# Groupnorm and attention on one core: scores of two rows in succession, and the order around them

## The reference

```python
x = x + attention(groupnorm(x))            # x: 16 images x 64 rows x 256 tokens x 128 channels, f32

groupnorm: mean and variance of each image over rows, tokens and the 4 channels of each of 32 groups
qkv   = einsum('bglc,dc->bgld', x, W_qkv) + b_qkv
score = softmax(einsum('bghlc,bghmc->bghlm', q, k) / sqrt(128))   # 2 heads of 64 channels, 256 x 256 each
out   = einsum('bghlm,bghmc->bghlc', score, v)
```

## Time and profile before

| | us |
|---|---|
| median of 3 runs | 3863.12 (3862.29 to 3874.12) |
| the profiled execution | 3873.13 |
| its span, first to last instruction | 3871.2 |
| PE busy | 3781.4 (98%) |
| DVE busy | 3778.0 (98%) |
| ACT busy | 3037.4 (78%) |
| POOL busy | 1787.6 (46%) |

### The profile page before, as it was taken

How to read it: one execution, slowest core, us unless ns; L and a number is a source line. 1 busy time by engine, 2 the same in 40 slices (tenths; PEclk the granted TensorE clock), 3 DMA queues, 4 the chain that set the end, 5 groups by cost and what they waited for, 6 DMA issues and landing times.

```text
span 3871.2 us, 126226 instructions
## 1 busy us (share of the span) xinstructions
PE 3781.4 (98%) x44133; PEld 2995.0 (77%) x44133; DVE 3778.0 (98%) x6114; ACT 3037.4 (78%) x8193; POOL 1787.6 (46%) x2065
## 2 busy tenths in 40 slices
PE   4999999999999999999999999999999999999998
PEld 2777777777777777777777777777777777777777
DVE  5999999999999999999999999999999999999999
ACT  2777888778888878778787877887878877888886
POOL 1444444444444444444444444444444444444444
PEclk9999999999999999999999999999999999999999
DMA  7999999999999999999999999999999999999999
GB/s 196 219 212 213 216 214 214 215 215 215 215 214 217 219 212 215 214 214 214 212 213 214 213 217 213 213 218 215 215 216 216 217 213 213 214 196 181 180 181 176
DMA packets 2442225, 813.91 MB, mean 210 GB/s; under 512 B 2179072, under 2 KB 2441600, under 8 KB 2441600
## 3 DMA queue, kind: packets, MB, share of 16 engines
q1 hardware_dynamic: 2311040, 679.97, 98.5%
q10 hardware_dynamic: 130560, 125.86, 12.5%
HBM read 134.42 MB, written 134.22 MB: 69 GB/s over the span
## 4 chain that ended last, share of the span: by engine, by line
PE 93%; DVE 2%; DMA 2%; issue 2%; POOL 1%; ACT 1%; SPq 0%; ACTq 0%; POOLq 0%; DVEq 0%
PE s_pair L271 27%; PE qk_bank L249 27%; PE o_bank L287 19%; PE v_bank L259 11%; PE xt_bank L241 6%; PE v_bank L256 3%; DMA pt_hi<-p_hi 1%; DVE first_bn L439 1%; DVE p_lo L410 1%; POOL p_hi L573 0%; ACT prob L367 0%; DVE neg_max L402 0%; DMA image<-in_x_dram 0%; SPq L207 0%; DVE o_norm L429 0%
## 5 line engine op out<-in xcount | busy, mean ns | idle before, releaser
L573 POOL TENSOR_SCALAR p_hi<-prob 128x1024 f16<-128x1024 f32 x1024 | 1073.1, 1048 | 2075.1 <-ACT prob L367 1827.4
L367 ACT ACTIVATE prob<-s_pair,neg_max 128x256 f32<-128x256 f32 x4096 | 1612.7, 486 | 18.3 <-issue 9.4
L410 DVE SCALAR_TENSOR_TENSOR p_lo<-prob,p_hi 128x1024 f16<-128x1024 f32 x1024 | 1477.4, 1443 | 50.6 <-POOL p_hi L573 26.3
L347 ACT ACTIVATE qk<-qk_bank,b_in 128x256 f32<-128x256 f32 x2048 | 860.3, 471 | 744.0 <-PE qk_bank L249 744.0
L402 DVE TENSOR_REDUCE neg_max<-s_pair 128x4 f32<-128x1024 f32 x1024 | 1238.6, 1210 | 20.3 <-PE s_pair L271 19.4
L271 PE MATMUL s_pair<-qk 64*128 64x256 f32 x8192 | 1164.5, 403 | 1.4 <-ACT qk L347 1.4
L249 PE MATMUL qk_bank<-xc,w_norm 128*128 128x256 f32 x4096 | 1160.7, 406 | 0.0
L249 PEld LDWEIGHTS qk_bank<-xc,w_norm 128*128 128x128 f32 x4096 | 695.3, 189 | 393.4 <-issue 335.6
L287 PE MATMUL o_bank<-v_hi,pt_lo 128*128 128x65 f16 x8192 | 850.2, 193 | 37.7 <-issue 25.5
L271 PEld LDWEIGHTS s_pair<-qk 64*128 64x128 f32 x8192 | 706.4, 186 | 220.0 <-issue 171.4
L287 PE MATMUL o_bank<-v_lo,pt_hi 128*128 128x65 f16 x8192 | 851.6, 194 | 0.0
(11 more groups left out here) (71 smaller groups left out, 1640.6 us busy)
## 6 DMA issues: line engine op xcount, KB each, us to landing
out_dram<-y_ring SPq DMA_DIRECT2D x512, 256.0 KB, 3.7
image<-in_x_dram ACTq DMA_DIRECT2D x480, 256.0 KB, 3.6
pt_hi<-p_hi SPq DMA_TRANSPOSE x1024, 4.1
pt_lo<-p_lo SPq DMA_TRANSPOSE x1024, 3.7
image<-in_x_dram SPq DMA_DIRECT2D x4, 2048.0 KB, 16.3
w_in<-in_L_conv_W_qkv_dram SPq DMA_DIRECT2D x1, 192.0 KB, 2.4
b_in<-in_L_conv_b_qkv_dram SPq DMA_DIRECT2D x3, 0.5 KB, 2.1
```

The lines of the kernel that those rows point to most:

```text
L347: ins = act.activation(qk[:, v % 2, t, :], qk_bank[:, t * TOK:(t + 1) * TOK], ACT.Identity, bias=b_in[:, t:t + 1])
L367: ins = act.activation(prob[:, m, c:c + TOK], s_bank[m][h][:, a * TOK:(a + 1) * TOK], ACT.Exp, bias=neg_max[:, m, h, a:a + 1])
L410: dve.scalar_tensor_tensor(out=p_lo[:, v % 2, :], in0=prob[:, v % 2, :], scalar=P_SCALE, in1=p_hi[:, v % 2, :], op0=ALU.mult, op1=ALU.subt ...
L573: pool.tensor_scalar(p_hi[:, v % 2, :], prob[:, v % 2, :], P_SCALE, 1.0, ALU.mult, ALU.mult).then_inc(phi_done, 1)
```

## The change

The diff, whole:

```diff
@@ -34,7 +34,7 @@
-    X_AHEAD = 2
+    X_AHEAD = 3
@@ -188,7 +188,7 @@
-                order(run, next_image)
+                order(run, next_image, i % 2)
@@ -221,10 +221,10 @@   (SP)
-            def order(run, next_image):
-                run(-2, transpose_low)
-                run(-7, store)
-                run(-1, transpose_high)
+            def order(run, next_image, odd):
+                run(-1, transpose_low)
+                run(-6, store)
+                run(0, transpose_high)
@@ -319,13 +319,15 @@   (PE)
-            def order(run, next_image):
-                run(0, scores)
-                run(+1, project_qk)
+            def order(run, next_image, odd):
+                if not odd:
+                    run(0, scores)
+                    run(+1, scores)
+                run(+2, project_qk)
                 run(0, project_v)
                 next_image(0)
                 run(-3, values)
-                run(+3, x_transpose)
+                run(+4, x_transpose)
@@ -375,12 +377,15 @@   (ACT)
-            def order(run, next_image):
+            def order(run, next_image, odd):
                 next_image(0)
-                run(-1, exponent, 0)
-                run(-1, exponent, 1)
-                run(+2, x_copy)
-                run(+1, qk_copy)
+                if not odd:
+                    run(+3, x_copy)
+                run(0, exponent, 0)
+                run(0, exponent, 1)
+                if odd:
+                    run(+3, x_copy)
+                run(+2, qk_copy)
                 run(0, v_high)
@@ -548,15 +553,18 @@   (DVE)
-            def order(run, next_image):
-                run(-2, p_low)
+            def order(run, next_image, odd):
+                if odd:
+                    run(0, row_max)
                 run(-4, sums)
                 next_image(0)
+                run(-4, divide)
+                next_image(1)
                 run(-1, v_low)
-                next_image(1)
-                run(-4, divide)
                 next_image(2)
-                run(0, row_max)
+                if not odd:
+                    run(0, row_max)
+                run(-1, p_low)
                 next_image(3)
                 next_image(MEASURE)
@@ -593,9 +601,12 @@   (POOL)
-            def order(run, next_image):
+            def order(run, next_image, odd):
+                if not odd:
+                    run(-4, finish)
                 run(0, p_high)
-                run(-4, finish)
+                if odd:
+                    run(-4, finish)
```

## The result

The changed kernel takes 4049.8 us (median of 4 runs, 4048.9 to 4052.5) against 3867.65 for the kernel before: 1.0473 times as long, 95% interval 1.0458 to 1.0488. That is 182 us more, where +133 was forecast (3996, on the median of 3863.12 known then).

The account below looks back on a forecast made before the run. The prediction took PE's own work to bound the kernel. 132 us for pairs with an even-step bn_stats, 11 for the others and -10 for hiccups gave +133, 3863.12 to 3996 us; range 3915 to 4055.

Parts of the forecast that it names:

- the signs that were named: PE idle at project_qk about 0.3 us and at project_v, pairs of 7.35 and 7.86, p_low's mean near 1.2.
- the forecast's own range: About 3925 to 4045 us, from errors in the sums' wait, pair lengths, hiccups and statistics.
- second circle: Even step with bn_stats: project_v waits for v_low behind DVE's two row maxima; pair 7.86 us, +0.55, 240 pairs, 132 us.
- hiccups: Irregular delays outside the steady steps; earlier loads and transposes were to save 10 us, bounds 0 and 25.
- first circle: Every pair: project_qk waits for qk_copy behind ACT's exponent; pair 7.35 us against 7.31, +0.04.
- 147 other pairs: Pairs outside rows 48 to 63 without an even-step bn_stats; +0.04 us each expected.
- statistics rows: Rows 48 to 63: more operations before v_low or row_max, some 0 to 15 us in all, taken as no difference.
- PE keeps the pace: Rival: no wait ends last, each pair takes the longer of PE's 6.96 and DVE's sum; about 3789 us, chance 0.05.
- Only ACT's circle holds: Rival: the bn_stats is hidden; 180 pairs at DVE's 7.54, others at 7.35; 3918 us, chance 0.09.
- a wash: Rival: ACT's circle alone, with the hiccups gone; 3858 us, chance 0.04.
- Contention comes back: Rival: finish slips onto p_low in the longer pairs, up to 0.54 us in 240 pairs; up to 4126, chance 0.08.

Follow-up runs that it names:

- e5: The changed kernel with v_low ahead of divide in odd steps only; even steps keep sums, divide, v_low: 3993.0 us.
- e2: The changed kernel with both bn_stats of a pair of steps at the end of the odd step: 3988.9 us.
- e4: The changed kernel with p_high casting 512 of 1024 columns from row 2 on, so part of the output is not computed: 4041.0 us.
- e9: The changed kernel with GpSimd's order as before the change, p_high then finish in even steps too: 4060.1 us.
- e3: The changed kernel with qk_copy of even steps between the two halves of the exponent on ScalarE: 4062.6 us.
- e11: e6 with statistics operations moved to even steps' ends or a row later, v_low before divide in every step, v_high earlier in odd and some even steps: 3885.5 us.
- e1: The changed kernel with v_low put back between sums and divide on VectorE in all steps: 4029.5 us.
- e6: The changed kernel with v_low before divide in odd steps, even steps' qk_copy between exponent halves, x_copy before the exponent in odd steps: 3931.9 us.

## Why the prediction was right, and where it was short

The direction and the mechanism held, and the signs that were named are there: PE idle for 0.29 us at project_qk behind qk_copy, project_v behind v_low, p_low's mean at 1.225. The sum was 49 us short (+133 against +182). The range held with 5 us to spare, and partly by luck: the forecast's own range ended at 4045, and only its stretch toward the rivals, to 4055, takes 4049.8 in.

*The second circle* was right to a few hundredths: 7.86 foretold, 7.90 measured. The bare wait between sums and divide, for which no row stood, was taken at 0.21 and is 0.21. e5 took the circle away and e2 its bn_stats, and both brought the time down, each to the next wait. That the sum agrees better still, 132 us foretold and 128.8 measured, is in part luck: the pairs got 0.58 longer by their medians (7.32 to 7.90), not 0.55, and the hiccups that went (below) took some of it back.

*The first circle* was in the right place and too short: 7.35 foretold, 7.45 measured. Of its steps the exponent came at 2.44 (2.42) and qk_copy at 3.88 (3.86); the step that failed is from the end of qk_copy to project_qk, 0.05 by the earlier trace rows and 0.14 here (1811.82 + 0.86 to 1812.82; 0.14 or 0.15 in all 482 such waits of this trace). Those rows were of scores that waited, not of project_qk. Why the one takes longer is open. The 147 other pairs were foretold 147 x 0.04 = 6 us and cost 16.5; 0.09 in each of them is 13, so this one step makes up what was lacking there (10.5).

*The statistics rows* are the term that was mis-sized. Their 120 pairs were foretold 120 x 0.04 = 5 us by the first circle and nothing for the operations ("some 0 to 15 us in all ... I take no difference"); they cost 34.9. At the 0.11 a pair that the other pairs cost, the first circle makes some 13 of it, an estimate, and the operations some 21. Two things were missed. In the changed kernel these operations stand in both circles, ahead of v_low(i) and of row_max(i), so what they take beyond the room there lengthens the pair. And they got longer, since p_high or finish now runs just then: 0.45 instead of 0.20 for the one shown. All of them in rows 48 to 63 took 78.7 us before and 113.2 in the changed kernel, 102.5 in e4, 127.6 in e9 and 141.4 in e3, and the sum of these pairs goes up and down with that. The prediction had looked at GpSimd's clash with p_low alone, and found rightly that it goes (1.443 to 1.225), but did not ask whom p_high and finish meet at their new times. The rule of the Trainium skill, SBUF — State Buffer, Who interferes with whom, which the prediction set beside p_low, speaks for these operations as well: two SBUF inputs against a GpSimd instruction that reads SBUF. e3's rows agree, 0.81 against 0.15.

*Hiccups:* 10 us were taken back for them, and about that much went, though no run separates it. Against the median of their group the pairs of the first and the third group ran over by 22 us in all before and by 8 in the changed kernel. POOL's waits for the transposes did not shrink with it: they grew from 192 to 231.6 us.

*The rivals.* "PE keeps the pace" needs row_max not to follow its own scores; the waits show that it does. Its floor was right to 0.04, though: 6.96, and 6.92 in e11. The Trainium skill's rule that changing the tiling mode drains TensorE (TensorEngine Tiling (Array Packing), Key Properties) agrees with the scores' 1.93 for two rows against 2.14, and was never what set the time. "Only ACT's circle holds" fell with the rows of DVE above, and "a wash" with the time. "Contention comes back" was right in kind and wrong in place: not finish on p_low, but p_high and finish on the statistics.

## What to carry to other kernels

When a stage is moved nearer to its source, lay out the loops that close over several engines, from one step's start to the next, with start-to-start times from rows in which the wait ended last; such a loop is a floor, however idle the engines on it are. An engine's gain counts only where no loop is longer than its own work. And when an edit is taken back and the time falls less than the loop says, look for the loop behind it: e1, e5 and e6 each found the next one, and e1 shows that one order can be right in even steps and wrong in odd ones.

## What the runs showed of the hardware

- A DVE operation on 128x32 tiles with both inputs in SBUF took 0.81 us instead of 0.15 when it began while GpSimd's p_high ran, and ended 0.04 us past its end (e3). In the changed kernel 44 of 90 such operations began beside p_high and ended 0.04 us past it, and 30 beside finish, 0.05 past it.
- From the end of qk_copy on ACT to the PE stage that waited for it: 0.05 us for scores and 0.14 for project_qk (changed kernel). What makes the difference was not tried.
- A division that waits for a reciprocal on the same engine (DVE) starts 0.21 us after the reciprocal's start, 0.04 past its end (0.17), in the changed kernel; before, with v_low between the two, v_low started 0.09 after the reciprocal.
